# Routing of the last half chunk laid over more gaps, and a tanh wait for GpSimd's products after the recurrence

## What is computed

```
scores = sigmoid(x @ router_w.T); sfc = scores + e_bias
group_scores = top_k(sfc in 8 groups of 8, 2).sum(-1)
keep the 4 best groups, then the 8 best experts in them
w = scores of the 8 / their sum * 2.5;  coef[t, e] = w or 0
g, u = x @ Wg[e], x @ Wu[e]
moe_out = sum over e of (silu(g) * u * coef[:, e]) @ Wd[e]   (+ a shared expert)
```

## Time and profile before

| | |
|---|---|
| median of 3 executions | 1079.64 us (1079.47 to 1080.21) |
| profiled execution, its own time | 1078.22 us |
| its span, first to last instruction | 1076.5 us |
| PE busy | 943.2 us, 88% |
| DVE busy | 732.7 us, 68% |
| POOL busy | 564.5 us, 52% |
| ACT busy | 478.1 us, 44% |
| mean granted TensorE clock | 0.890 |
| coefficient load, issue to landing, median | 3.9 us |
| tail, from the tanh of unit 78 to that of unit 131 | 506.87 to 630.46 us |

### The profile page before, as it was taken

How to read it: one execution, slowest core, us unless ns; L and a number is a source line. 1 busy time by engine, 2 the same in 40 slices (tenths; PEclk the granted TensorE clock), 3 DMA queues, 4 the chain that set the end, 5 groups by cost and what they waited for, 6 DMA issues and landing times. The chain is left out here.

```text
span 1076.5 us, 29797 instructions
## 1 busy us (share of the span) xinstructions
PE 943.2 (88%) x12378; PEld 631.0 (59%) x12378; DVE 732.7 (68%) x1789; ACT 478.1 (44%) x889; POOL 564.5 (52%) x519
## 2 busy tenths in 40 slices
PE   3598987699999999999989968889999899998786
PEld 3377776455555555555434426677777667776554
DVE  5635455557676767767866656778787777777664
ACT  2232223132323233233222216677777677775652
POOL 3688801033434343434545555666766666667763
PEclk9555555589999999999999988999999999998998
DMA  9120024232222222322344410000000000000001
GB/s 251 34 74 1 2 50 86 57 84 76 63 80 65 79 60 80 82 62 79 98 103 118 118 39 2 2 2 3 3 3 3 2 3 3 3 3 2 2 2 40
DMA packets 46205, 51.68 MB, mean 48 GB/s; under 512 B 22102, under 2 KB 36727, under 8 KB 46071
## 3 DMA queue, kind: packets, MB, share of 16 engines
q1 hardware_dynamic: 43152, 48.78, 17.6%
q10 hardware_dynamic: 2918, 1.01, 0.5%
HBM read 48.20 MB, written 1.57 MB: 46 GB/s over the span
## 5 line engine op out<-in xcount | busy, mean ns | idle before, releaser
L712 POOL TENSOR_TENSOR ex<-ex,xn 128x512 f32<-128x512 f32 x128 | 162.4, 1269 | 224.2 <-ACT thcb L960 109.3
L960 ACT ACTIVATE thcb<-ps 128x512 f32<-128x512 f32 x132 | 78.9, 598 | 207.0 <-PE ps L1787 206.0
L793 POOL TENSOR_TENSOR wu<-encC,wu 128x1024 f16<-128x1024 f32 x64 | 137.4, 2161 | 57.8 <-ACT encC L1028 57.8
L1794 PE MATMUL ps<-ex,wd 128*128 128x512 f32 x256 | 138.8, 625 | 0.5 <-DVE xT L1385 0.5
L1373 DVE SCALAR_TENSOR_TENSOR ex<-thcb,ps 128x512 f32<-128x512 f32 x132 | 90.6, 686 | 59.6 <-ACT thcb L960 55.6
L1787 PE MATMUL ps<-xnT,wg 128*128 128x512 f16 x384 | 105.3, 383 | 2.1 <-DVE ex L1379 2.0
L1732 PEld LDWEIGHTS ps<-eb,encC 128*128 128x128 f16 x3072 | 86.8, 99 | 32.1 <-DVE eb L1242 19.5
L1787 PE MATMUL ps<-xnT,wu 128*128 128x512 f16 x384 | 104.1, 380 | 0.0
L1021 ACT CAST wu<-ps 128x1024 f16<-128x1024 f32 x64 | 64.9, 1015 | 85.1 <-PE ps L1878 85.1
L787 POOL TENSOR_TENSOR wd<-wd,a_sum 128x512 f32<-128x512 f32 x64 | 66.5, 1042 | 67.2 <-DVE a_sum L1494 67.2
L1843 PE MATMUL ps<-wg,M 128*128 128x128 f16 x1536 | 97.3, 221 | 2.1 <-DVE wg L1463 2.1
(11 more groups left out here) (309 smaller groups left out, 1792.7 us busy)
## 6 DMA issues: line engine op xcount, KB each, us to landing
xn<-coef_rows SPq DMA_DIRECT2D x128, 256.0 KB, 3.9
thcb<-in_L_ffn_Wg SPq DMA_DIRECT2D x8, 256.0 KB, 3.2
thcb<-in_L_ffn_Wu SPq DMA_DIRECT2D x8, 256.0 KB, 3.3
wd<-in_L_ffn_Wd SPq DMA_DIRECT2D x2, 1024.0 KB, 10.2
xtok<-in_x SPq DMA_DIRECT2D x4, 256.0 KB, 6.1
thcb<-in_ctx SPq DMA_DIRECT2D x2, 512.0 KB, 11.3
wu<-in_L_xcond_attn_wq SPq DMA_DIRECT2D x2, 512.0 KB, 11.0
wu<-in_L_xcond_attn_wk SPq DMA_DIRECT2D x2, 512.0 KB, 10.6
```

The costliest lines, as they stand in the source:

```text
L712: nc.gpsimd.tensor_tensor(hid[:, side(m, n), :], gu[:, side(m, n), :], other, ALU.mult)\
L793: nc.gpsimd.tensor_tensor(z[:, 1, 8 * u:8 * u + 8, :], a_Zc[:, u], z[:, 0, 8 * u:8 * u + 8, :], ALU.subtract)\
L960: nc.scalar.activation(th[:, side(m, n), :], bank(side(m, n)), ACT.Tanh, scale=0.5 / WSCALE)\
L1794: mm(bank(5), wd[:, n, :] if n < PAIRS else swd[:, :], hid[:, side(m, n), :], start=(n == 0), stop=(n == UNITS - 1)).then_inc(s["y_ready"], 1)
```

## The change

The last part gets a table of its own, LAST, and the product in the tail gets the wait that place 1 has in the recurrence, for every unit but the very last.

```diff
+        LAST = {0: ("project",), 2: ("residual",), 3: ("stats",), 6: ("x1T",), 8: ("xn2T",), 10: ("router",), 12: ("sig0",),
+                13: ("sig1",), 14: ("sfc",), 15: ("halves",), 17: ("quarters",), 18: ("pairs",), 19: ("top2",), 21: ("more",),
+                22: ("equal",), 23: ("rank",), 25: ("under",), 26: ("mask",), 27: ("pick",), 28: ("take0", "take1"),
+                30: ("sum",), 31: ("inverse",), 32: ("coef",), 33: ("coefT",)}
+        PARTS[-1] = PARTS[-1][:4] + (LAST,)
...
                     elif place == 3 and t + 1 < T:
                         pool.wait_ge(s["en_ready"], t + 2)
+                    elif t >= T and (m, n) != chunk_units[-1]:
+                        pool.wait_ge(s["th_ready"], m * UNITS + n + 2)
                     unit(m, n)
```

## The result

| | before | changed |
|---|---|---|
| median of 4 executions | 1079.56 us (1078.63 to 1080.21) | 1069.13 us (1068.65 to 1070.93) |
| profiled execution, its own time | 1078.22 us | 1070.93 us |
| its span | 1076.5 us | 1069.2 us |
| tail, tanh of unit 77 to tanh of unit 131 | 127.07 us | 121.21 us |
| ahead of it, from the tanh of unit 0 | 281.67 us | 283.45 us |

A forecast was written before the change was run, and what follows sets the result against it. PE's matmuls bound plain units at 2.153 us, so only longer units could gain: -3.5 - 3.0 + 0.6 = -5.9 us, profiled 1078.22 to 1072.3, plus 1.42 for the median: 1073.7 us, 80% range 1072.0 to 1077.0.

The forecast's parts named there:

- The wait: Tail: products start some 0.07 us after the next tanh, wholly beside a pass, and cost plain units nothing.
- The slots: Last part on DVE: routing instructions starting within 0.87 us of the slot's begin are free; only the last csum step is caught.
- Term one: Units 88 to 93: the 3.53 us lost to DVE's lateness go, all of it; bounds 2.5 and 3.53.
- coefT: PE's transposes of the coefficients: a wait of 0.96 us, 1.2 of 4.23 us remaining if the clock holds.
- Term two: Unit 93 to 94, PE's wait for coef: 3.0 of 4.23 us go; bounds 1.5 and 4.0.
- case B: Clock falls to its lower level after the 0.96 us at coefT: gain 4.4 us, time 1075.2; chance 0.10.
- The head: Units 78 and 79: normalisation and next product start later behind the waiting product, 0.6 us lost; bounds 0 and 0.9.
- The work behind the tail: From the last down matmul's end: one chain that moves up as it is.
- A: DVE falls out of step, late passes feeding themselves over slots 7 to 12: gain 3.0 us, time 1076.6; chance 0.15.
- C: Csum step not caught, coef on time for PE: gain 6.9 us, time 1072.7; chance 0.10.
- D: Slower: products beside passes take above 1.99 us, so 53 units each pay; at 2.1, time 1085.4; chance 0.03.
- E: The change does nothing that counts, for instance through a second cause of the last part's lateness: 1079.6; chance 0.04.

The follow-up runs named there:

- wait_only: The changed kernel with only the tanh wait of the products and the old table HALF for the last part: median 1076.43 us, ratio 0.9979 to the kernel before.
- head_free: The changed kernel without the tanh wait for unit 78's product: tail 120.71 us, median 1070.53 us, ratio 0.9936 to the kernel before.
- better: head_free with inverse moved to offset 32, coef to 33, coefT to 35: tail 119.54 us, median 1067.38 us, ratio 0.9914 to the kernel before.

## Why the prediction was right in the tail and wrong in the time

- What bounds: right. Every plain unit took 2.15 us in all kernels, and no change made it shorter.
- The wait: right. Products start 0.88 us after the last one ended, released by the tanh, and take 1.27 beside a pass; the coefficient loads and the down matmuls of plain units cost nothing.
- The slots: right in each for this table, the caught csum step too, forecast to start at 0.15 and found at 0.17 us behind the product's start. Term one, 3.53, is gone whole. The margin was drawn too wide: 0.87 was free by the prediction, and an instruction at 0.85 was caught in wait_only, where the product started 0.82 into the slot. For this table that changed nothing, since no last start lay between.
- coefT: right. Forecast a wait of 0.96, measured 0.99; 1.2 of 4.23 us to remain, 1.40 remained. Term two is 2.8, not 3.0. The clock held, so case B did not come.
- The head: right. Forecast 0.6, measured 0.50 by head_free.
- The sum of the tail: forecast 5.9, measured 5.86 in the first pair of traces and 6.0 in the later ones.
- "The work behind the tail ... is one chain from there, so it moves up as it is": this is the step that failed. The instructions move up as they are, their duration doesn't: stretches at the lower clock fall on them differently at another time, and where they slow the attention's score matmuls, DVE's addition starts after GpSimd's subtraction and takes 1.7 to 2.6 us for 0.68. The runs showed 440.3 to 446.0 us for the work behind the tail, where the prediction had a constant. The prediction knew this catching and looked for it in the tail alone. Why the changed kernel gains a lasting 2.7 us there stays open. The other 1.8 of the 10.4 us come from the sample: the forecast started from 1079.64, on the upper side of the executions of the kernel before. The range took its bounds from the tail's rivals alone and had nothing for this, although the three executions and the profiled one already stood 1.4 us apart.
- Rivals: A is real, and came where the table was left out (wait_only). C did not come, and better is what it would have given, with the 0.5 us of the head besides; D and E did not come.

## What to carry to other kernels

Where an engine's small instructions with two SBUF inputs meet another engine's long SBUF instruction, let a semaphore start the long one together with work of the first engine that reads PSUM, and cut the small work into pieces whose last instruction starts before that: here neither the wait (0.9 us) nor the new table (3.1 us, where moving coefT only gave 3.5) was worth what both were (6.0 us). When a kernel is made shorter in the middle, put a few us on the range of the forecast for stages that only move in time, look there for pairs of instructions on the two engines whose order hangs on 0.2 us, and compare stage by stage in the trace before crediting a change with the whole difference.

## What was not expected of the hardware

One program on one chip took from 1071.0 to 1083.2 us without any change in its instructions. A delay of 1.1 us on the chain that the attention waits for did not make the kernel slower by the medians in either of two trials. Being late by 0.03 us cost an instruction on 128 x 16 numbers 1.1 us, after which the lateness renewed itself in later slots. And behind the tail a few tenths of a us more on 48 matmuls, 1.82 us where 1.80 still did nothing, lengthened a DVE instruction from 0.68 to 2.64 us, by letting GpSimd's start 0.04 us ahead of it.
